# Score and value matmuls of a step issued alternately in a graph attention kernel (float32, one core)

## What is computed

```
h = jnp.maximum(_layernorm(x, axis=-1), 0.0)
q = h @ Wq.T + bq;  k = h @ Wk.T + bk;  v = h @ Wv.T + bv
a = q @ k.T * scale + adj + adj
x = x + softmax(a, axis=-1) @ v
```

## Time and profile before

| | us |
|---|---|
| median of 3 runs | 823.91 |
| lowest, highest | 822.46, 825.2 |
| the profiled execution | 823.64 |
| its span | 821.8 |
| TensorE busy | 807.6 (98%) |
| VectorE busy | 587.8 (72%) |
| ScalarE busy | 361.2 (44%) |
| GpSimd busy | 382.8 (47%) |

### The profile page before, as it was taken

The page is one execution under the profiler, slowest core; times in us unless marked ns, Lnnn a source line. Parts: engine busy times, 40 slices in busy tenths (PEclk is TensorE's granted clock), DMA queues, the critical chain, the costliest instruction groups (busy, mean ns, idle before and its releaser), DMA issues.

```text
span 821.8 us, 16591 instructions
## 1 busy us (share of the span) xinstructions
PE 807.6 (98%) x6702; PEld 805.4 (98%) x6702; DVE 587.8 (72%) x980; ACT 361.2 (44%) x651; POOL 382.8 (47%) x329
## 2 busy tenths in 40 slices
PE   7899999999999999999999999999999999999998
PEld 6899999999999999999999999999999999999988
DVE  4687777677777777777777777777777777777753
ACT  3684434434443343444334444434444444444364
POOL 2463908263360727346071724618182451818272
PEclk9999999999999999999999999999999999999999
DMA  6350324334332433334243333323333332333200
GB/s 223 114 182 26 104 78 129 91 91 116 91 109 72 130 92 99 106 91 116 67 126 101 93 104 92 115 76 118 103 91 111 90 108 83 111 103 98 84 26 14
DMA packets 43852, 81.68 MB, mean 99 GB/s; under 512 B 4992, under 2 KB 5632, under 8 KB 43776
## 3 DMA queue, kind: packets, MB, share of 16 engines
q1 hardware_dynamic: 43344, 80.10, 33.2%
q10 hardware_dynamic: 432, 0.53, 0.2%
HBM read 76.42 MB, written 4.19 MB: 98 GB/s over the span
## 4 chain that ended last, share of the span: by engine, by line
PE 97%; DVE 1%; ACT 1%; DMA 1%; issue 0%; POOL 0%; ACTq 0%; DVEq 0%
PE ps L309 50%; PE ps L395 15%; PE ps L397 15%; PE ps L396 15%; PE ps L301 1%; DMA w_all<-in_w 1%; PE ps L382 0%; PE ps L375 0%; ACT x_third L460 0%; PE ps L328 0%; PE ps L324 0%; DVE x_res L620 0%; DVE hT L562 0%; POOL v L263 0%; ACT v_full L478 0%
## 5 line engine op out<-in xcount | busy, mean ns | idle before, releaser
L309 PE MATMUL ps<-qhl,hT 128*128 128x256 f32 x3072 | 407.5, 282 | 1.2 <-POOL v L263 1.2
L309 PEld LDWEIGHTS ps<-qhl,hT 128*128 128x128 f32 x3072 | 384.4, 190 | 1.4 <-POOL v L263 1.4
L281 POOL TENSOR_TENSOR ring_a<-ring_a,m_row 128x512 f32<-128x512 f32 x179 | 230.2, 1332 | 215.4 <-ACT m_row L523 215.4
L395 PE MATMUL ps<-v,p_hi 128*128 128x258 f32 x1024 | 291.1, 284 | 1.2 <-DVE x_res L620 1.2
L397 PE MATMUL ps<-v,p_lo 128*128 128x258 f32 x1024 | 288.9, 282 | 0.0
L396 PE MATMUL ps<-v,p_hi 128*128 128x256 f32 x1024 | 288.7, 282 | 0.0
L519 ACT CAST p_hi<-ps 128x512 fp32r<-128x512 f32 x256 | 150.4, 588 | 246.3 <-PE ps L397 244.2
L577 DVE TENSOR_TENSOR ring_a<-ps,ring_a 128x512 f32<-128x512 f32 x179 | 123.4, 689 | 102.3 <-PE ps L309 101.5
L395 PEld LDWEIGHTS ps<-v,p_hi 128*128 128x128 f32 x1024 | 194.0, 189 | 1.4 <-DVE x_res L620 1.4
L397 PEld LDWEIGHTS ps<-v,p_lo 128*128 128x128 f32 x1024 | 194.1, 190 | 0.0
L396 PEld LDWEIGHTS ps<-v,p_hi 128*128 128x128 f32 x1024 | 193.3, 189 | 0.0
(11 more groups left out here) (74 smaller groups left out, 362.9 us busy)
## 6 DMA issues: line engine op xcount, KB each, us to landing
ring_a<-in_adj SPq DMA_DIRECT2D x179, 256.0 KB, 2.7
ring_b<-in_adj SPq DMA_DIRECT2D x77, 256.0 KB, 2.7
x_res<-in_x SPq DMA_DIRECT2D x16, 256.0 KB, 3.0
out<-x_res SPq DMA_DIRECT2D x16, 256.0 KB, 2.0
x_pair<-in_x SPq DMA_DIRECT2D x5, 512.0 KB, 3.8
x_third<-in_x SPq DMA_DIRECT2D x2, 512.0 KB, 3.7
w_all<-in_w ACTq DMA_DIRECT2D x2, 256.0 KB, 3.9
x_pair<-in_x SPq DMA_DIRECT2D x4, 128.0 KB, 4.0
```

The lines of the kernel that those rows point to most:

```text
L281: nc.gpsimd.tensor_tensor(slot_tiles(w), slot_tiles(w), m, ALU.subtract).then_inc(s_sub, 1)
L309: last = nc.tensor.matmul(dst, lhs(a, ib), rhs(c, ib), start=(n == 0), stop=(n == 3 * DB - 1))
L395: nc.tensor.matmul(ps[:, O_BANK + i, 0:VW], hi, v[:, n, 0:VW], start=(n == 0), stop=False)
```

## The change

The 12 score matmuls and the 12 value matmuls of a step are issued alternately, one score and one value, and not first all scores and then all values. What either waits for is waited for ahead of all 24. The transposes of `turn_max` and `spread_max` and the matmuls of `project_q` stood between scores and values; they now stand behind both. Within the values the order of the 12 is another one too: the bank changes at every matmul (query tile 0, query tile 1), where it changed at every third. In steps with only one of the two kinds the scores run as before, and the values in the new order of their own.

```diff
+    MATMULS = 3 * DB * KT
...
-            def scores(s):
+            def scores_ready(s):
                 b, u = s // UNITS, s % UNITS
                 if u == 0:
                     pe.wait_ge(s_qlo, b + 1)
                 if s >= 2:
                     pe.wait_ge(s_add, s - 1)
-                for k in range(KT):
-                    at = (KT * u + k) * P
-                    last = split_product(ps[:, S_BANK + s % 2, k * QB:(k + 1) * QB],
-                                         lambda a, ib: hT[:, a, ib, at:at + P],
-                                         lambda c, ib: qhl[:, b % 2, c, ib, :])
-                last.then_inc(s_score, 1)
+
+            def score_matmul(s, n):
+                b, u = s // UNITS, s % UNITS
+                k, n = n // (3 * DB), n % (3 * DB)
+                ib, (a, c) = n // 3, ((0, 0), (0, 1), (1, 0))[n % 3]
+                at = (KT * u + k) * P
+                last = nc.tensor.matmul(ps[:, S_BANK + s % 2, k * QB:(k + 1) * QB], hT[:, a, ib, at:at + P],
+                                        qhl[:, b % 2, c, ib, :], start=(n == 0), stop=(n == 3 * DB - 1))
+                if k == KT - 1 and n == 3 * DB - 1:
+                    last.then_inc(s_score, 1)
+
+            def scores(s):
+                scores_ready(s)
+                for n in range(MATMULS):
+                    score_matmul(s, n)
...
-            def weigh_values(w):
+            def values_ready(w):
                 b, u = w // UNITS, w % UNITS
                 if u == 0 and b > 0:
                     pe.wait_ge(s_fin, b)
                 pe.wait_ge(s_plo, w + 1)
-                for k in range(KT):
-                    n = KT * u + k
-                    for i in range(QS):
-                        hi = p_hi[:, w % PB, k, i * P:(i + 1) * P]
-                        lo = p_lo[:, w % PB, k, i * P:(i + 1) * P]
...
-                last.then_inc(s_pv, 1)
+
+            def value_matmul(w, n):
+                u = w % UNITS
+                k, part, i = n // (3 * QS), n % (3 * QS) // QS, n % QS
+                t = KT * u + k
+                side = p_lo if part == 2 else p_hi
+                columns = slice(VW, VW + D) if part == 1 else slice(0, VW)
+                last = nc.tensor.matmul(ps[:, O_BANK + i, 0:D if part == 1 else VW],
+                                        side[:, w % PB, k, i * P:(i + 1) * P], v[:, t, columns],
+                                        start=(t == 0 and part == 0), stop=(t == TILES - 1 and part == 2))
+                if n == MATMULS - 1:
+                    last.then_inc(s_pv, 1)
...
             for s in range(FIRST, STEPS + LAG + len(HOLD)):
                 b, u = s // UNITS, s % UNITS
+                w = -1 if s in HOLD else due(s)
                 if s < STEPS:
-                    scores(s)
+                    scores_ready(s)
+                if w >= 0:
+                    values_ready(w)
+                for n in range(MATMULS):
+                    if s < STEPS:
+                        score_matmul(s, n)
+                    if w >= 0:
+                        value_matmul(w, n)
                 if u == 0 and b <= BLOCKS:
                     turn_max(b - 1)
                 if u == 1 and b <= BLOCKS:
                     spread_max(b - 1)
                 if u == UNITS // 2 and b + 1 < BLOCKS:
                     project_q(b + 1)
-                if s not in HOLD and due(s) >= 0:
-                    weigh_values(due(s))
```

## The result

The changed kernel takes 857.01 us (median of 4 runs, 856.01 to 859.87) against 823.18 us for the kernel before on the same chip: a ratio of 1.0421, 95% interval 1.0394 to 1.0448. Forecast were 858.8 us and 4.2% slower. The profiled execution of the changed kernel has a span of 854.2 us.

What follows compares the result with a forecast made beforehand. TensorE, busy 98% of the span, was taken as the bound: matmul count times pace. Stalls of 26.9 + 6.0 + 0.9 + 1.4 = 35.2 us on 823.64 gave 858.8 us, 4.2% slower; range 845 to 868.

Steps and rivals of the forecast that it cites:

- `finish`, each of 14: Steps at a block's first unit: TensorE waits uncovered for finish, behind add_adj; 1.92 us each, 26.9 us in all.
- behind project_q, each of 14: Second step after project_q: write_p_lo ends late, TensorE waits; 0.43 us each including restart, 6.0 us in all.
- step 22, once: At the start, the first values wait for write_p_lo(0) at the head of the step: 0.9 us with restart.
- start of the tail, once: At step 256 turn_max stands behind the values and the next values wait for write_p_lo: 1.4 us.
- pace of the mixed matmuls: In 233 mixed steps, 4427 more bank changes: between -7 and +7 us, taken as 0.
- The rival at 805 us: Back-to-back bank alternation frees the pace of 5592 mixed matmuls to 0.11 us, saving 54 us; chance 0.03.
- The low bounds, 846 us: TensorE issues across the wait or finish comes sooner: stalls 1.44 us, 22.5 us in all; chance 0.08.
- The restart: After a stall TensorE's second matmul comes 0.22 and not 0.12 us later: 0.10 us more per stall.
- u = 2: Third step of a block: running_max over two SBUF tiles, GpSimd now beginning after VectorE; taken as 0, bound 3.4 us.
- The rival at 895 us: Stalls bring TensorE's clock down: 24 matmuls at half pace behind each of 14, 36 us more; chance 0.04.
- The argument from the 1.18 us gap of the tail: Against the clock falling: behind this gap the second matmul is 0.22 us later, the following again 0.12 apart.
- Slack of an ordinary step: VectorE chains have 0.73 us to spare, no cost; rival without that slack 882 us, chance 0.05.

Runs made afterwards that it cites:

- the value order alone: Kernel before with only the 12 value matmuls in the changed kernel's order, bank changing at each: 823.13 us, ratio 1.0007.
- the covers kept: Changed kernel, scores first and undivided in finish steps, those before, u = 8, steps 22 and 255; tail transposes ahead of values: 822.13 us, ratio 0.9992.
- the waits alone: Changed kernel without alternation: both waits ahead, then 12 scores, then 12 values, transposes and project_q behind both: 851.44 us, ratio 1.0351.
- with `finish` ahead: Changed kernel with finish on VectorE just ahead of the add_adj of the step before: 852.5 us, ratio 1.0361.
- only the first was undone: Changed kernel, but in the 14 steps where values wait for finish the scores come first, undivided: 838.33 us, ratio 1.0191.
- the run with every cover kept: Changed kernel, scores first and undivided in finish steps, those before, u = 8 and step 22, but step 255 still interleaved: 823.47 us, ratio 1.0014.
- the run with project_q ahead: Changed kernel with project_q ahead of the 24 interleaved matmuls of its step, not behind them: 854.27 us, ratio 1.0382.
- the longer `finish`: Changed kernel with one more VectorE operation in finish, ahead of the two that write x_res: 874.17 us, ratio 1.0628.

## Why the prediction was right

Term by term, from the distances of starts in the profile after. The sum is measured from the first spreading to the end:

| term | forecast | measured |
|---|---|---|
| `finish`, each of 14 | 1.92 | 1.93 |
| behind project_q, each of 14 | 0.43 | 0.54 |
| step 22, once | 0.9 | 1.0 |
| start of the tail, once | 1.4 | 1.4 |
| pace of the mixed matmuls | 0 | -1.2 |
| sum | 35.2 | 35.7 |

The last row is closer than its parts: project_q cost 1.5 us more than forecast in all, and the pace gave 1.2 back. That these two cancel is luck; `finish`, three quarters of the sum, was right by its mechanism. The medians of the timed runs differ by 33.8 us, with preludes of their own lengths in them.

**The pace.** The earlier trace rows said that a change of bank is worth nothing, and the runs bear it out from both sides: the value order alone at 1.0007, the covers kept at 0.9992. The rival at 805 us has fallen. The mean distance of ordinary starts is 118.80 ns before, 118.85 with the value order alone, 118.59 after: what little the pace won didn't come with the bank changes among the values.

**finish.** The two causes were told apart. That the wait stands ahead of all matmuls costs 1.45 us (the runs with the waits alone and with `finish` ahead, 1.2 us idle each); `add_adj` in front of it costs 0.49. That the second exists shows where only the first was undone: 0.49 of each stall stayed, and the time was 838, not 830 us. The low bounds, 846 us, would have wanted a matmul issued across the wait, or `finish` ahead of `add_adj`; neither came in the kernel after, and where a run put `finish` ahead a stall cost about 1.45 us instead of 1.93.

**project_q.** The chain was right to 0.01 us: 3.27 us from its last matmul (345.42) to the end of p_lo (348.69). The semaphore was mis-sized: 0.14 us from p_lo to the matmul, where I had taken 0.05. That is what the wait for `finish` has in the tail of the kernel before, `x_res` complete at 794.96 by its trace and TensorE's matmul at 795.01; behind `finish` in the kernel after it is 0.10. The restart is 0.08 and not 0.10.

**u = 2.** I took the maximum over two ring slots at its short length, since GpSimd would begin behind it. That is so:

```profile
322.75 0.70 DVE L605 TENSOR_TENSOR ps<-ring_a 128x512 f32<-128x512 f32 x1
322.81 6.81 POOL L282 TENSOR_TENSOR ring_a<-ring_a,m_row 128x512 f32<-128x512 f32 x5 [23.11 <-ACT m_row L541]
```

It lasts 0.70 us where the earlier trace rows has 1.79: GpSimd starts 0.06 us after it and not 0.05 before. So it is in 14 blocks of each kernel, and over all 13 profiles the operation takes 1.8 us where GpSimd starts 0.03 to 0.06 us ahead of it, and 0.70 where GpSimd starts behind. A tenth of a microsecond in the order of two engines moved 1.1 us of VectorE's time, here to no effect on the end.

**The clock.** The rival at 895 us didn't come, but it was nearer than its 4% said. At 1.70 us idle none of 14 stalls brought the clock down; at 1.86, in the run with every cover kept, the one did, and at 2.03 seven of 14. The size was off as well: 16 matmuls at half pace, 1.5 us, not a whole step of 24 at 2.6. The argument from the 1.18 us gap of the tail couldn't carry over to 1.7. A nearer row was in the trace of before, and the prediction has no place for it: its prelude has TensorE idle for 1.85 us between two full stretches. The same pause stands in the prelude of every profile, and in that of the run with project_q ahead the clock falls behind it. First the kernel before, then that run, each with the pause and the stretch behind it (granted clock third from the right):

```profile
31.18 1.09 PE L301 MATMUL ps<-ident,x_third 128*128 128x128 f32 x8 [1.85 <-ACT x_third L460]
31.20:34.50 3.30, 3.30 (x29) 3.30 (x30) 1.14 (x1) 1.79 (x3) 1.08 (x2) 1.00 0.31 72
```

```profile
31.09 1.94 PE L302 MATMUL ps<-ident,x_third 128*128 128x128 f32 x8 [1.85 <-ACT x_third L478]
31.20:34.50 3.30, 3.30 (x16) 3.30 (x17) 0.38 (x1) 1.02 (x1) 0.98 (x2) 0.50 0.19 32
```

It falls so in 4 of 12 profiles with that pause, and in the 13th, where it is 1.96 us, it doesn't. One profile of before couldn't show that; its row alone would have spoken for the forecast. The earlier trace rows is weaker evidence than it was taken for: it shows a pace of 0.227 us, while the page of before grants 9 tenths in that slice. The run with the longer `finish` shows both together, 0.214 us at a granted 0.50.

**Slack of an ordinary step.** No wait in ordinary steps; the waits of the kernel after are the ones listed.

## What to carry to other kernels

Before a finer order of two streams is tried, ask what the coarse order hid: here each block of 12 undivided matmuls was the cover of a chain on another engine, and the wait that was pulled to the head of the step took the cover away. Where a wait exists in some steps only (a block's end, a projection), look at those steps one by one; the ordinary step has slack and shows nothing. If two streams are to be mixed, keep them apart in the steps in which one of them must wait, and in the step ahead of it.

## What was not expected of the hardware

- Matmuls over 128 columns with weights of their own can start 0.06 us apart, but their weight loads don't start less than 0.108 us apart, so that three of mixed width take 0.34 us, against 0.36 for three over 256 columns.
- The granted clock falls to half for about 3.4 us (16 matmuls at 0.214 us) behind some pauses of 1.85 us and more in an otherwise full TensorE: 5 of 13 at 1.84 to 1.86 us (12 in preludes, one in a tail), none of one at 1.96, 7 of 14 at 2.03, every second; none of 14 at 1.70 in the kernel after, and none of 14 in the run with project_q ahead. In the run with the longer `finish` a further 0.34 us of stall so costs 1.1 us.
- After the stalls looked at the second matmul comes later than the pace: by 0.08 us where the first is a score matmul, by 0.10 to 0.11 where it is a value matmul.
